# One-core graph-transformer kernel: attention units as scores, transposes, context with the projections in one block

## What is computed

```
xn = layernorm(x)
x  = x + relu(segment_sum((xn @ W)[src] * edge_w, dst)) + linear_attention(xn)      # 20000 edges
q, k, v = (layernorm(x) @ Wq + bq), ...        # 8 heads of 64
attn = softmax(q k^T / 8);  h = layernorm(. + attn v @ Wo + bo)
e = argmax(h @ gate_W + gate_b);  x = x + gate * (gelu(h @ W1[e] + b1[e]) @ W2[e] + b2[e])   # 8 experts, 2048 wide
for l in range(2):                              # graph attention over the same edges, 8 heads
    a = softmax over the edges of q[dst] . k[src], times v[src]
    y = batchnorm(y + a @ Wo[l].T + bo[l]);  y = batchnorm(y + relu(y @ W1[l].T + b1[l]) @ W2[l].T + b2[l])
x  = x + layernorm(y) + a second linear attention
x  = x + sum over top 2 of 8 experts of gelu(w * h @ W1 + b1) @ W2
```

## Time and profile before

| | us |
|---|---|
| median of 3 runs | 1137.46 |
| lowest, highest run | 1136.33, 1140.64 |
| span of the profiled execution | 1134.8 |
| chain's share on PE | 84% |
| window loop (lines 682 to 696) | 43 to 120 |
| PE from the end of the windows (120) to the mask `cnt_adj` (DVE, line 1547, at 172.3) | busy 52.0 of 52 |
| attention 0 | 233 to 376 |
| experts | 406 to 634 |
| attention 1 | 648 to 785 |
| attention 2 | 846 to 986 |

### The profile page before, as it was taken

The page is one execution under the profiler, slowest core; times in us unless marked ns, Lnnn a source line. Parts: engine busy times, 40 slices in busy tenths (PEclk is TensorE's granted clock), DMA queues, the critical chain, the costliest instruction groups (busy, mean ns, idle before and its releaser), DMA issues.

```text
span 1134.8 us, 20059 instructions
## 1 busy us (share of the span) xinstructions
PE 1087.0 (96%) x7339; PEld 728.6 (64%) x7340; DVE 560.2 (49%) x1409; ACT 371.2 (33%) x931; POOL 126.9 (11%) x183
## 2 busy tenths in 40 slices
PE   3899999999999988999999899999999999999999
PEld 2588646468777554455545577887577778755764
DVE  7999738645445421121211444553324455587641
ACT  1012212035555412122212445453124455412630
POOL 1045460020000020010101530000000000001000
PEclk9999999999999999999999999999999999999999
DMA  4100475000000379800899840000210100000001
GB/s 133 38 1 3 131 201 213 1 28 29 19 11 1 155 248 409 332 14 18 330 400 403 295 167 29 29 29 1 75 56 29 29 29 1 1 37 1 1 3 43
DMA packets 21402, 112.69 MB, mean 99 GB/s; under 512 B 5127, under 2 KB 6904, under 8 KB 15198
## 3 DMA queue, kind: packets, MB, share of 16 engines
q1 hardware_dynamic: 15864, 100.95, 23.7%
q0 software_dynamic: 5472, 10.83, 3.6%
HBM read 102.78 MB, written 8.98 MB: 98 GB/s over the span
## 4 chain that ended last, share of the span: by engine, by line
PE 84%; DMA 5%; DVE 5%; issue 2%; ACT 2%; POOL 1%; DVEq 1%; SPq 0%; POOLq 0%
PE psum L624 11%; PE psum L805 10%; PE psum L1002 7%; PE psum L979 6%; PE psum L828 6%; PE psum L692 6%; PE psum L859 6%; PE psum L810 5%; PE psum L841 5%; PE psum L1129 3%; PE psum L1033 3%; DMA arena<-in_moeW 3%; PE psum L642 3%; PE psum L1107 3%; PE psum L762 2%
## 5 line engine op out<-in xcount | busy, mean ns | idle before, releaser
L624 PE MATMUL psum<-arena 128*125 128x512 f32 x320 | 140.0, 593 | 0.8 <-ACT arena L1203 0.7
L1233 ACT ACTIVATE arena<-arena,small 125x625 f32<-125x625 f32 x120 | 97.0, 809 | 89.9 <-DVE small L1622 89.9
L805 PE MATMUL psum<-arena 128*128 128x313 f32 (+1 forms) x384 | 110.0, 435 | 2.3 <-ACT arena L1171 1.4
L1308 ACT ACTIVATE arena<-psum,cols 128x64 f32<-128x64 f32 x224 | 47.4, 358 | 183.3 <-PE psum L988 183.3
L624 PEld LDWEIGHTS psum<-arena 128*125 128x125 f32 x320 | 59.2, 187 | 73.7 <-issue 69.6
L979 PE MATMUL psum<-arena 128*64 128x512 f32 x448 | 99.2, 594 | 6.1 <-DMA arena<-in_moeW 4.4
L1002 PE MATMUL psum<-arena 128*64 128x256 f32 x896 | 100.4, 381 | 3.0 <-DMA arena<-in_moeW 2.9
L805 PEld LDWEIGHTS psum<-arena 128*128 128x128 f32 x384 | 69.9, 189 | 31.2 <-ACT arena L1171 2.5
L1622 DVE CUSTOM_DVE_ANT_0 arena<-psum,cnt_adj 125x625 f32<-125x625 f32 x80 | 61.5, 806 | 55.0 <-PE psum L828 55.0
L1241 ACT ACTIVATE arena<-psum 125x500 f32<-125x500 f32 x120 | 63.8, 583 | 73.2 <-PE psum L841 73.2
L1002 PEld LDWEIGHTS psum<-arena 128*64 128x64 f32 x896 | 63.1, 137 | 36.3 <-issue 4.5
(11 more groups left out here) (299 smaller groups left out, 1422.2 us busy)
## 6 DMA issues: line engine op xcount, KB each, us to landing
arena<-in_moeW SPq DMA_DIRECT2D x32, 2048.0 KB, 18.2
arena<-in_att SPq DMA_DIRECT2D x36, 256.0 KB, 2.7
arena<-in_l1W SPq DMA_DIRECT2D x2, 2048.0 KB, 11.2
token_rows<-arena POOLq DMA_DIRECT2D x19, 128.0 KB, 4.9
rows<-in_rows SPq DMA_DIRECT2D x1, 2240.0 KB
expert_rows<-arena POOLq DMA_DIRECT2D x17, 128.0 KB, 4.8
arena<-in_gnnWo SPq DMA_DIRECT2D x2, 1024.0 KB, 5.6
arena<-token_rows POOLq DMA_DIRECT2D x14, 128.0 KB, 6.8
```

Of the source, the lines that this page charges most:

```text
L624: mm = pe.matmul(bank(b, NP, D), srcT[:, k, c * NP:(c + 1) * NP], w[:, k, :], start=(k == 0), stop=(k == KC - 1))
L805: mm = pe.matmul(bank(b, P, width), aw[:, w, k, :], srcT[:, k, o:o + width], start=(k == 0), stop=(k == KC - 1))
L1233: act.activation(Sx[u % 3][h], Sx[u % 3][h], ACT.Exp, bias=small[0:NP, 80 + n:81 + n], scale=-1.0, accum_out=small[0:NP, 120 + n:121 + n]) ...
```

## The change

1. In an attention PE's order in step u becomes `scores(u + 2)`, `turned(u)`, then for c = 2 (`BLOCK`) all six projections of the next pair, then `context(u - 1)`. The last two units (`LAST` = 18) keep the old order. ACT does `turned_out(u)` in step u, and all four `projected` at c = 2; DVE both `values` at c = 2.
2. Each transpose of 125x125 becomes two pieces, of 64 and of 61 rows (`QROWS`), which lie in the two halves of the array's rows, as the scores do: 20 pieces per unit for 10 transposes. The pieces of a half go to a bank of its own (3 and 4), the fifth columns to bank 7 (5 for the last units), which the projections use too; hence the waits on `vc`, `low` and, ahead of projection 1, `pTc`.
3. An expert tile's 8 transposes of 128x128 become 16 pieces of 64 rows, in banks 2, 3, 6 and 7, each half preceded by a product with one column.
4. The window sums: ACT copies the three parts to three places (`WT`, `w_mids`, `cnt_adj`) with three instructions per window for one, and POOL adds them once after the last window, in two instructions of 3125 elements for 38 smaller ones. DVE waits for the first add ahead of `mk` and for the second ahead of the mask.
5. The ends of the window loops are masked with `END_BITS`: one register instruction more per turn and one more per window, on PE and on DVE.
6. More constant products before the experts: three of half width for one, one of half width more, and 3 for 2 in two places.

```diff
-    def fill(b, n):
+    def fill(b, n, width=D):
...
-                    fill(b, 1)
+                    fill(b, 3, D // 2)
...
-            fill(b, 2)
+            fill(b, 3)
...
-            return [0] + list(first), second
+            return [0] + [end & END_BITS for end in first], second
...
-                if w >= 2:
-                    act.wait_ge(wt_out, w - 1)
-                act.activation(parts[w % 2], sums[:, :, 0:3 * DW], ACT.Copy).then_inc(parts_out, 1)
+                for v, part in enumerate([WT, w_mids, cnt_adj]):
+                    i_ = act.activation(part[:, :, DW * w:DW * w + n], sums[:, :, DW * v:DW * v + n], ACT.Copy)
+                i_.then_inc(parts_out, 1)
...
+            pool.wait_ge(parts_out, NW)
+            pool.tensor_tensor(WT, WT, w_mids, ALU.add).then_inc(wt_out, 1)
+            pool.wait_ge(wt_out, 1)
+            pool.tensor_tensor(WT, WT, cnt_adj[:], ALU.add).then_inc(wt_out, 1)
...
                 def turned(u):
+                    def piece(g, h, j):
+                        r0, r1 = QROWS[g]
+                        o = 512 * (3 + g) + 64 * (4 * h + j) if j < 4 else 512 * tails_bank(u) + 64 * (2 * h + g)
+                        return pe.transpose(psum[0:NP, o:o + r1 - r0], Sx[u % 3][h][r0:r1, j * NP:(j + 1) * NP],
+                                            ident[r0:r1, r0:r1])
...
+                    for j in range(4):
+                        piece(0, 0, j)
+                        piece(1, 0, j)
...
                     if u + 2 < PAIRS * NC:
                         scores(u + 2)
-                    if i + 1 < PAIRS:
-                        for n in ((0, 1), (2,), (3,), (4,), (5,))[c]:
+                    if u < LAST:
+                        turned(u)
+                    if c == BLOCK and i + 1 < PAIRS:
+                        for n in range(6):
+                            if n == 1:
+                                pe.wait_ge(s["pTc"], 3 * (u + 1))
                             projection(i + 1, n)
...
                     if u:
                         context(u - 1)
-                    turned(u)
+                    if u >= LAST:
+                        turned(u)
```

More of the change, by code:

```diff
@@ L222, in build @@
         bounds = take(1, WMIN, dt=I32)
-        parts = [at(o_T + 2 * KC * N + i * NC * 3 * DW, NP, NC, 3 * DW) for i in range(2)]
+        w_mids = at(o_T + 2 * KC * N + D, NP, NC, N)
+        assert o_T + 2 * KC * N + D + NC * N <= o_N + NC * D
         assert oa[0] <= o_cnt
@@ L313, in build @@
             A.append({n: sem(f"att{a}_{n}") for n in (
-                "wq", "wk", "wv", "proj", "qk", "vc", "tail", "score", "max", "exp", "sum", "prob", "pT", "pTc",
+                "wq", "wk", "wv", "proj", "qk", "vc", "tail", "score", "max", "exp", "sum", "prob", "low", "pT", "pTc",
                 "av", "ctx")})
@@ L515, in _ @@
             pool.memset(twos[:], 2.0).then_inc(consts, 1)
-            pool.memset(gateW[:, KC * EX:], 0.0).then_inc(consts, 1)
-            pool.memset(gateW1[:, KC * EX:], 0.0).then_inc(consts, 1)
+            for h in range(2):
+                o = 2 * KC * EX + h * (WMIN // 2)
+                pool.memset(gates[:, o:o + WMIN // 2], 0.0).then_inc(consts, 1)
             pool.memset(zero_rows_sb, 0.0).then_inc(consts, 1)
@@ L668, in _ @@
             pe.wait_ge(range_ready, 1)
[L669 removed]
+            ends, shifts = window_ranges(pe, mybir.EngineType.PE)
             def window_banks(w):
@@ L909, in gate_chunk @@
                 return mm
-            def fill(b, n):
+            def fill(b, n, width=D):
                 for _ in range(n):
-                    pe.matmul(bank(b, P, D), onesf[0:NP, :], rows[:, 0, :], start=True, stop=True)
+                    pe.matmul(bank(b, P, width), onesf[0:NP, :], rows[:, 0, 0:width], start=True, stop=True)
             product_chunk("ao", T2, ring[5 % 2], 3)
@@ L955, in _ @@
             pe.nop().then_inc(M["y"], 1)
-            def tile_columns(n):
-                pe.wait_ge(M["xs"], n * 16)
-                pe.matmul(bank(5, P, 1), xs[:, 0:P], ident[0:TT, 0:1], start=True, stop=True)
-                for k4 in range(KC):
-                    mm = pe.transpose(bank(5, P, TT, TT * k4), xs[:, k4 * P:(k4 + 1) * P], ident[0:TT, 0:TT])
-                mm.then_inc(M["xsT"], 1)
             with pe.Fori(0, EX // 2) as i:
@@ L1259, in attention @@
                         exponentials(u + 2)
-                    if i + 1 < PAIRS:
-                        for n in ((0, 1), (2,), (3,), (), ())[c]:
+                    if c == BLOCK and i + 1 < PAIRS:
+                        for n in range(4):
                             projected(i + 1, n)
@@ L1307, in _ @@
                                 f = b * (FC // 2) + q * 4 + j4
-                                done = act.activation(hT[:, f, :], bank(2 + b, P, TT, P * j4 + TT * q),
+                                done = act.activation(hT[:, f, :], bank(HT_BANKS[b][q], P, TT, TT * j4),
                                                       ACT.Gelu_apprx_tanh,
@@ L1508, in _ @@
             ve.wait_ge(range_ready, 1)
-            ends, shifts = window_ranges(mybir.EngineType.DVE)
+            ends, shifts = window_ranges(ve, mybir.EngineType.DVE)
             for w in range(NW):
```

126 lines of the change are left out of this document (77 added, 49 removed).

## The result

| | before | changed |
|---|---|---|
| median, us | 1139.0 | 1156.15 |
| lowest, highest | 1136.33, 1140.64 | 1154.79, 1157.84 |
| span of the profiled execution | 1134.8 | 1156.2 |
| own time of that execution | not given | 1157.84 |

The ratio is 1.0146, with a 95% interval of 1.0128 to 1.0164: slower, as forecast, but above the range (1132 to 1153): 17.2 us between the medians, where the sum had 7.1. Beside the later kernels the one before took 1139.1 to 1139.9 us, so its trace, with 1134.8, is one of its quicker executions; part of the 21.4 us between the two spans is that.

A forecast was written before the change was run, and what follows sets the result against it. PE was taken as the bound, with 84% of the chain that ended last. Attentions 11.1, experts -2.9, windows -1.7 and constant products +0.6 gave +7.1 us, put on the median 1137.46: 1144.6 us, range 1132 to 1153.

The forecast's parts named there:

- the sum: Whole kernel: attentions 11.1, experts -2.9, windows -1.7, constant products +0.6, together +7.1 us.
- the forecast's walk: Attentions: the three engines' queues worked through in order; units every 16.6, 3.6, 4.7, 3.9, 4.5 us; +3.7 per attention.
- the price taken between 65 and 212: Attentions: a pair of pieces takes 107 ns, the load's pace with both halves at once; ends 65 and 212.
- (a): Attentions: half-height pieces load fast, a pair takes 65 ns; -6.4 us in all, 1131 us; chance 0.18.
- (c): Attentions: pieces go one behind the other at 106 ns, three attentions lose 51 us; 1184 us; chance 0.06.
- (b): Attentions and windows: waits smaller than worked out, or register instructions hidden; about 1138 us, within 5.7; chance 0.28.
- scores wait for `max` 2.3 us per five units: Attentions: scores wait for DVE's maximum in units without projection, three times, 7.0 us per attention.
- 2.9 us: Start of an attention: turned(0), scores(3) and scores(4) find nothing ready where projections stood; 2.9 us lost.
- the old wait of 0.3: Attentions: a wait in the kernel before that goes with the change, -0.3 us per attention.
- -1.7: Windows: 6.7 us gained without POOL's adds, 5.0 given back to register instructions; between -6.7 and +1.
- the forecast's own sign (1.95 to 2.05): Window loop: turns at 1.95 to 2.05 us show the register instructions, 1.86 would show them hidden.
- -2.9 for the stage: Experts: 0.34 us less per tile, -4.7 over 14 tiles, 5 or 6 struck for weight waits; between -5 and +2.

The follow-up runs named there:

- e3: Changed kernel with two constant products of 512 columns ahead of scores(3) in each attention, filling PE's wait: 1152.92 us, ratio 1.01.
- e10: Changed kernel with one constant product in the wait at each attention's start: 1150.72 us, ratio 1.0104.
- e7: Changed kernel with the whole old order in the attentions on all three engines, but transposes as 64-row pieces: 1138.8 us, ratio 0.9988.
- e9: Changed kernel with projections spread, new order and pieces for units 0 to 14, old order with full transposes for the last pair: 1130.51 us, ratio 0.9923.
- e8: Kernel before with part 5 (END_BITS) alone: 1141.82 us, ratio 1.0015.
- e5: The changed kernel run once more, unedited: 1155.98 us, ratio 1.0142.
- e1: Changed kernel with the attentions of the kernel before (parts 1 and 2 undone, the rest kept): 1137.09 us, ratio 0.997.

## Why the prediction was wrong, and where it was right

**The sign and the mechanism were right.** Slower, by waits on DVE's `largest` that take the place of projections. Units without projection come within 0.2 us of the forecast's walk, and the twenty pieces take 1.17 us, 109 ns a pair, for 107: the price taken between 65 and 212. Rivals (a) and (c) fall by that. The reason given for the price is not shown, and the price is partly luck. The prediction set 189 ns for loads of 125 columns against 141 for 128, as if the columns made the difference, but the page of before has 189 ns for 128 columns too:

```profile
L805 PEld LDWEIGHTS psum<-arena 128*128 128x128 f32 x384 | 69.9, 189 | 31.2 <-ACT arena L1171 2.5
```

And 109 ns a pair is also what two pieces would take one behind the other at 54 ns each, near the pace of the experts' pieces (below). (b) was right in part: the waits on DVE are 8.1 us for 9.9, and the register instructions 1.0 for 5.0, but the other terms below took that back.

**What failed is a term that the sum did not have.** Every wait was priced at its own length, "scores wait for `max` 2.3 us per five units" and "2.9 us" at the start, with TensorE's clock taken as it was before. The wait at the start, 1.86 us long, pulled the clock down to 1.2 GHz at 8 of 9 such places. That cost 2.7 and 4.2 us in the first trace, 8.3 in the second, and it was gone in e3 and e10, where two constant products and one stand in the wait. The profile of before gave a hint only: its waits in the experts, 2.3 us at the longest, had no such stretch behind them, and the prediction does not mention the clock. Of the 14.3 us by which the spans differ more than the sum said, the clock in the attentions is 6.9, the attentions at full clock 2.0, the experts 2.5 (with a stretch at 1.2 GHz of their own), the start 2.0, the windows 1.0, and the rest about nothing.

**The attentions at full clock: 13.1 us for 11.1.** From the first scores to the last an attention takes 115.0 us for 111.6, by the starts of its scores in attention 0. The waits on DVE are 8.1 us there, all on the scores, where the forecast had 9.9. The work fell by 8.1 - 3.4 = 4.7, where the forecast had 6.3 with the old wait of 0.3. The six projections in one block take 730.97 - 717.96 = 13.0 us, so that the entries there are saved as forecast. The two misses, 1.8 and 1.6, nearly cancel, which is luck. The rest of the 4.4 is 1.0 us behind the last scores, which the forecast did not look at: it "worked the three queues through" for the units alone. e7 shows the same place 1.5 us longer with pieces in the old order, and e9, with the old transposes there, 21.1 us in attention 0 as before.

**Windows: -0.7 for -1.7, and both halves were too large.** In the total the register instructions cost 1.0 us (e8: 77.6 for 76.6) where 5.0 were put, and part 4 of the change, POOL's adds above all, gave back 77.6 - 75.9 = 1.7 where 6.7 were put. A late turn of the changed kernel takes what an early one did; below it, three turns in a row, before and now:

```profile
113.07 1.85 PE L705 MATMUL psum<-arena 125*128 x30
...
63.04 5.57 PE L692 MATMUL psum<-arena 125*128 x90
...
59.89 5.75 PE L705 MATMUL psum<-arena 125*128 x90 [0.17 <-DVE arena L1559]
```

So the late turns' length was the effect of POOL's adds, as forecast, but few turns had it. The price of a register instruction was right: 5.75 - 5.57 = 0.18 us at two borders between turns, 0.09 each. Up to the start of the seventeenth turn it shows, 32.3 us in e8 for 31.0; over the rest of the turns e8 takes no more than the kernel before (43.4 for 43.5), so it was hidden there, and behind what is not shown. From turn to turn the changed kernel takes 2.04 us (median, for 1.93), which by the forecast's own sign (1.95 to 2.05) is the instructions showing.

**Experts: the middle as forecast, by luck, and the sum not.** Between the layers of a tile:

```profile
521.45 0.27 PE L1019 MATMUL psum<-ident,arena 64*128 64x1 f32 x1
521.46 0.33 PE L1024 MATMUL psum<-ident,arena 64*128 64x64 f32 x2
...
521.63 0.50 PE L1024 MATMUL psum<-ident,arena 64*128 64x64 f32 x6
521.97 0.41 PE L1030 MATMUL psum<-ident,arena 64*128 64x64 f32 x4
...
522.92 1.30 PE L1042 MATMUL psum<-arena 128*64 128x256 f32 x10
```

1.47 us for 1.78, forecast 1.44. But the pieces do not go in pairs at 65 ns, 33 for one: six of them take 521.97 - 521.63 = 0.34 us, 57 ns each. What makes up for it is the one-column product, whose records lie among the first pieces: the two together take 521.97 - 521.45 = 0.52 us, where the sum had 0.24 + 0.26. Tiles whose weights are there come every 15.4 us for 15.7, and the last ten of the thirteen steps from tile to tile are together 2.9 us shorter. The first three, in which PE waits for rows and weights, take 55.0 us before, 56.6 in the changed kernel and 54.3 in its second trace (e5). The stage took 230.6 us for 231.0, and between 229.1 and 234.0 in the traces that have the new tile, 232.5 and 233.8 in two that have the old. The first tile waits for its rows between nothing and 3.5 us:

```profile
422.32 0.26 PE L1019 MATMUL psum<-ident,arena 64*128 64x1 f32 x1 [3.52 <-DMA arena<-token_rows]
```

for 1.31 before, mostly with a stretch at 1.2 GHz behind it. So the gain per tile is shown; with this spread the -2.9 for the stage is neither shown nor refuted. All parts but the attentions together gave a ratio of 0.997 in e1.

**The start, 2.0 us later, does not belong to the change.** In the change it is the products of line 637 that are longer:

```profile
23.49 19.08 PE L637 MATMUL psum<-arena 128*125 128x512 f32 x40
```

for 17.43 before, the first four of them at half the pace of the rest. Five of the fourteen traces have it so (19.1 to 19.4 us, four or five of the products at half pace), e8 with part 5 alone among them, and nine have 17.43, e5 with the whole change among them. In the thirteen other traces the windows start between 43.6 and 46.5 us.

**POOL's two long adds were hidden, as forecast**: 6.8 and 6.9 us for 8, and the stage behind the windows takes 123.0 us as before. What they cost DVE was mis-sized: four two-input operations took 4.50, 5.82, 1.52 and 1.52 us, together 11.4 more than at 0.48 each, where 8 times 1.0 was put; the cover was long enough for that too.

**Constant products**: the gates' stage took 30.2 us for 30.1, where +0.6 was put.

**The range** failed by 3 us, and it failed for want of the clock's term: with 3 us for each of three stretches, its upper end would have been 1162. With the wait covered, e3 and e10 (1152.92 and 1150.72) stand inside it as it was. Its lower end was put loosely: it is said to take in most of (a) and to leave out half of it, and (a)'s own 1131 lies below it.

## What to carry to other kernels

A wait put on TensorE is worth its own length only while it leaves the clock alone; price it once at full clock and once with the stretch at 1.2 GHz behind it (here 1.4 to 4.2 us, at waits of 1.86 and 2.66), look for such stretches in the granted clock, and where there is one put a product in the wait that nobody reads. Work that keeps an engine busy while others go round is cover: gather it in one place and every other place is bare. When an order saves entries, keep the old order at the end and at the start, where nothing covers the latency, and change it only between; e9 shows this for the end, and for the start it was not tried.

## What the hardware showed that was not expected

- Ten pairs of pieces, 64 and 61 rows in the two halves of the array, took as long as ten transposes of 125 rows, 109 ns a pair and 109 ns a transpose: half the height saved nothing. Whether the two halves ran at once, or one behind the other in half the time, is not shown; the experts' pieces, in two halves as well, start 57 to 62 ns apart, and the input transposes, all in one half, 62.
- Going from scores to pieces cost no entry (units of 5.88 us for 6.08), going from pieces to scores left a unit at 6.01, a third of it by a wait of 0.07 us, though both lie alike in the rows.
- A two-input DVE operation that takes 0.48 us took 5.82 beside one long POOL add:

```profile
122.28 6.80 POOL L540 TENSOR_TENSOR arena<-arena 125x3125 f32<-125x3125 f32 x1 [117.33 <-ACT cnt_adj L1224]
...
124.92 4.50 DVE L1571 TENSOR_TENSOR arena<-arena 128x312 f32<-128x312 f32 x1
...
129.15 6.92 POOL L542 TENSOR_TENSOR arena<-arena,cnt_adj 125x3125 f32<-125x3125 f32 x1
...
130.60 5.82 DVE L1571 TENSOR_TENSOR arena<-arena 128x313 f32<-128x313 f32 x1 [0.15 <-ACT arena L1231]
```

It ended at 136.42, 0.35 us behind the add, and the one before it, 4.50 us long, ended at 129.42, 0.34 us behind the first add: each waited for the whole instruction. Beside the five shorter adds these operations take 1.50 before and 1.52 here. The forecast used that 1.50. The Trainium skill (GPSIMD Engine Reference, 1. Specifications) names the cause: POOL shares its way into SBUF with DVE instructions that have two SBUF inputs; the trace agrees, and shows that the length of POOL's instruction sets the price.
- Behind a wait of 2.66 us TensorE ran at 1.2 GHz for 3.4 us; with the 1.86 us of the changed attentions, with pieces and small waits after it, for 3.4 to 10.2.
- Transposes alone brought TensorE from 1.2 to 2.4 GHz at the kernel's start (their pitch went from 207 to 106 ns).
